# Layer 0 of a fused transformer kernel: the dense pieces of the batches start at slot 13 of the loop in place of slot 1

## The reference, cut to what matters

```python
xn = _layernorm(x, axis=-1)
x = x + _L0_attn_ref(xn, wq, wk, wv, wo) + _L0_ffn_ref(xn, ...)
xn = _layernorm(x, axis=-1)
x = x + _L1_attn_ref(xn, ...) + _L1_ffn_ref(xn, ...)
```

```python
x = fwht(x * SU_ug) / SCALE
x_up = x @ W_up.T * (Wscale_ug[:INTER] * SCALE)          # INTER = 1024
x_gate = x @ W_gate.T * (Wscale_ug[INTER:] * SCALE)
x = silu(x_gate) * x_up
x = fwht(x * SU_dp) / SCALE
x = x @ W_down.T * (Wscale_dp * SCALE)
```

## Time and profile before

| what | us |
|---|---|
| median of 3 runs | 1179.88 (1179.0 to 1183.53) |
| the profiled execution | 1184.52 |
| its span, first to last instruction | 1182.7 |
| PE busy | 1087.1 (92%) |
| DVE busy | 704.8 (60%) |
| ACT busy | 655.8 (55%) |
| POOL busy | 459.1 (39%) |
| mean granted TensorE clock | 0.974 of 2.4 GHz |

### The profile page before, as it was taken

One profiled execution on the slowest core, in us unless ns is written; L12 is line 12 of the kernel. 1 busy time (PEld: TensorE's weight loads), 2 busy tenths in 40 slices (PEclk: granted clock), 3 DMA queues, 4 the chain that ended last, 5 costly groups with the idle time before them and its releaser, 6 DMA issues. The chain is left out here.

```text
span 1182.7 us, 25082 instructions
## 1 busy us (share of the span) xinstructions
PE 1087.1 (92%) x7605; PEld 667.5 (56%) x7606; DVE 704.8 (60%) x2445; ACT 655.8 (55%) x1340; POOL 459.1 (39%) x525
## 2 busy tenths in 40 slices
PE   6679999999999999998879669999999999999985
PEld 3345666666666656663655425555555555555564
DVE  6486656656656666661228836566565656566566
ACT  4214455555555544446243738777877787787720
POOL 4323231322222000000330047777677777777510
PEclk9799999999999999999899979999999999999997
DMA  7500131113111310101110675484557646676277
GB/s 237 98 9 12 30 52 30 31 31 51 31 30 31 48 25 22 22 2 56 36 36 6 166 172 177 142 264 152 179 169 236 191 137 201 189 228 228 76 267 284
DMA packets 81681, 129.65 MB, mean 110 GB/s; under 512 B 32777, under 2 KB 53002, under 8 KB 81035
## 3 DMA queue, kind: packets, MB, share of 16 engines
q1 hardware_dynamic: 61576, 76.94, 23.3%
q0 software_dynamic: 15360, 47.21, 13.0%
q10 hardware_dynamic: 4616, 3.91, 1.2%
HBM read 97.57 MB, written 30.05 MB: 108 GB/s over the span
## 5 line engine op out<-in xcount | busy, mean ns | idle before, releaser
L684 DVE CUSTOM_DVE_ANT_0 a_masked<-a_ps_s,a_mask 128x512 bf16<-128x512 f32 (+3 forms) x512 | 229.9, 487 | 160.4 <-PE a_ps_s L843 156.6
L600 ACT ACTIVATE a_probs<-a_ps_e 128x512 f32<-128x512 f32 (+1 forms) x384 | 188.3, 527 | 122.6 <-PE a_ps_e L863 121.6
L1854 PE MATMUL e_ps_gu<-e_w_gu,e_xT 128*64 x640 | 208.6, 469 | 1.1 <-DVE e_xT L1724 1.1
L189 POOL DMA_INDIRECT yn<-rows,inv x160 | 162.1, 1013 | 122.3 <-DVE inv L1404 60.5
L1854 PE MATMUL e_ps_gu<-e_s_gu,e_xT 128*64 128x352 f32 x640 | 208.6, 469 | 0.0
L1633 POOL DMA_INDIRECT y<-e_y,dst x160 | 161.3, 1008 | 60.5 <-issue 28.9
L1879 PE MATMUL e_ps_y<-e_w_d,e_hT 88*64 x640 | 151.4, 379 | 0.9 <-DVE e_hT L1749 0.9
L1879 PE MATMUL e_ps_y<-e_s_d,e_hT 88*64 88x256 f32 x640 | 151.4, 379 | 0.0
L843 PE MATMUL a_ps_s<-a_kT,a_qT 72*128 72x512 bf16 (+3 forms) x512 | 131.3, 301 | 13.9 <-DVE a_headmax L684 11.1
L860 PE MATMUL a_ps_e<-a_qT,a_kT 75*128 75x512 bf16 (+3 forms) x512 | 140.8, 303 | 2.1 <-ACT a_probs L600 1.8
L1854 PEld LDWEIGHTS e_ps_gu<-e_w_gu,e_xT 128*64 128x64 f32 x640 | 81.7, 137 | 90.6 <-issue 90.6
(11 more groups left out here) (243 smaller groups left out, 1888.6 us busy)
## 6 DMA issues: line engine op xcount, KB each, us to landing
e_w_gu<-e_gu SPq DMA_DIRECT2D x64, 352.0 KB
e_w_d<-e_down SPq DMA_DIRECT2D x64, 176.0 KB
a_qT<-qk_parts SPq DMA_DIRECT2D x48, 192.0 KB
e_w_gu<-y SPq DMA_DIRECT2D x12, 768.0 KB, 6.6
qk_parts<-a_stage SPq DMA_DIRECT2D x16, 256.0 KB, 2.6
e_w_gu<-y SPq DMA_DIRECT2D x4, 1024.0 KB, 7.8
qkv<-y SPq DMA_DIRECT2D x12, 256.0 KB
yn<-rows,inv POOLq DMA_INDIRECT x160, 3.7
```

What stands on the lines that cost most here:

```text
L189: eng.indirect_dma_start(self.x[:, j % self.NS, :], None, t["rows"], bass.IndirectOffsetOnAxis(inv[:, j:j + 1], 0)).then_inc(self.x_in[j % ...
L600: nc.scalar.activation(probs[:, i % HKV, UCOL[u]:UCOL[u + 1]], ps_e[:, (i * 3 + u) % 2, 0:w], ACT.Exp, scale=SCALE0).then_inc(exp_done, 1)
L684: ins = V.tensor_tensor_reduce(masked[:, n % 2, c:c + w], ps_s[:, n % 2, c:c + w], mask[:, T - w:T], 1.0, -3e38, ALU.add, ALU.max, headmax ...
L1854: ins = nc.tensor.matmul(ps_gu[r * SEG:(r + 1) * SEG, j % 2, 0:2 * INTER1], xT[:, j // 2 % 2, j % 2, k * P + r * SEG:k * P + (r + 1) * SEG ...
```

## The change

`FFN0` is the slot of the first dense piece, `NX` the number of `xnT` buffers (2 KB of each partition more). Nothing else differs.

```diff
@@ -202,9 +202,9 @@
         STEPS = HEADS // HKV
         LAG, END = 12, HEADS + 12 + 5
         EARLY, OWN = TPB + 1, TPB
-        FFN0 = 1
+        FFN0 = 13
         HALF = T // 2
-        NQ, NV, NX = 3, 3, 3
+        NQ, NV, NX = 3, 3, 4
         STEPS_R, NS_ = 7, NP_ * 2 + 2
         RQ = MROW + NP_
```

## The result

The changed kernel took 1193.8 us (median of 7 runs, 1189.6 to 1198.0), the kernel before 1183.3 on the same chip (7 runs, 1179.0 to 1185.1). The ratio is 1.0101, 95% interval [1.0081, 1.0121], that is +11.9 us [9.6, 14.3]. Forecast were +8.8 and a ratio of 1.0075, just under the interval: right in direction, too small in size. The profiled execution took 1193.77 (span 1191.9).

The account below looks back on a forecast made before the run. TensorE was busy 92% of the span; VectorE set the pace in slots 2 to 7. Terms −11 + 4.3 + 3.0 − 2.6 + 13.7 + 0.8 + 0.6 = +8.8 us, on 1179.9 giving 1188.7; range 1182.5 to 1196.

Parts of the forecast that it names:

- Head: Slots 1 to 11 lose eleven dense pieces: −11 us, between 13.4 gained at full clock and 8.6 at low clock.
- VectorE sets the pace: Slots 2 to 7 of the old head: VectorE busy 22.1 of 24.0 us, TensorE 17.9.
- Slots 12 to 16: Three more pieces at 2.15 us each, the table load and the clock behind the head: +7.9 us.
- Clock behind the head: Slots 12 and 13 run slow if the clock is low at slot 12: 0 to 2.5 us, taken as +0.6.
- table load: ScalarE's load moves to slot 12's first exponential, where key scores wait: 0 to 1.3 us, taken as +0.8.
- rival 1: The head keeps the full clock, −13.4 there and nothing at slots 12 and 13: +5.8 us, 1185.7; chance 0.27.
- Slots 17 to 127: One piece fewer, fronts in free slots and shorter load waits together: −1.7 us.
- Fronts in free slots: A tile's transpose, parts and projection, formerly behind down slots, now in free ones: +0.7 us each, +3.0 in all.
- load waits: Maximum scores waiting for q and k at slots 32 and 96 get more time: −2.6 us, bounds 0 and −2.6.
- the price of a piece: Two more dense pieces in slots 12 to 127, put at 2.15 us each: +4.3.
- Tail: Nine slots, 128 to 136, go from 2.03 to 3.55 us by a closed gate-up loop: +13.7 us.
- Rivals 2 and 3: First: dearer tail and boundaries, about +15 us, chance 0.16. Second: the tail hides its pieces, +1 us, chance 0.07.

Follow-up runs that it names:

- e6: The changed kernel with idle matmuls that nobody reads at the end of slots 0 to 12 and the table loaded ahead of the loop: 1185.8 us, ratio 1.0045.
- e10: The kernel before with its last dense half at slots 128 to 139 and two of VectorE's down-weight operations moved to ScalarE: 1178.0 us, ratio 0.9962.
- e5: The changed kernel again, unaltered, for more runs and a second profile: 1192.3 us, ratio 1.0099.
- e3: The changed kernel with one exponential ahead of the loop, so that ScalarE loads its table early: 1192.9 us, one run.
- e1: The kernel before with the fourth xnT buffer alone: 1182.6 us, ratio 0.9998.
- e4: The kernel before with only the last dense half moved, from slots 113 to 124 to slots 128 to 139: 1179.2 us, ratio 0.9967.
- e2: The changed kernel with idle matmuls that nobody reads behind the units of slots 0 to 7: 1191.1 us, ratio 1.0075.
- e7: The changed kernel with the first dense piece at slot 9: 1190.0 us, one run.
- e9: The kernel before with the last half at slots 128 to 139, halves 1, 3 and 5 four slots later, and four buffers: 1179.1 us, ratio 0.9969.

## Why the prediction missed the size

- **Head, −11 forecast, −10.8 measured, in part by luck.** VectorE's ten slots from 2 to 12 took 88.75 − 58.20 = 30.55 us, between the 27.4 reckoned for the full clock and the 32.2 for the low one. The reason given was off: I had the clock come back with slots 10 and 11, and it stayed at 0.50 there (slot 11 took 4.22). The low clock cost the head about 3.8 us (slots 2 to 11 took 32.5, and 28.7 with the fillers of e6), not the 2.4 charged; but the gain at the full clock would be about 14.6 (an estimate, 10.8 + 3.8), not 13.4, and the two errors cancel. "VectorE sets the pace" was half the reading (e10), without harm, since the sum took VectorE's own rows.
- **Slots 12 to 16, +7.9 forecast, +7.3 and +9.9 measured. This is the step that failed:** "Clock behind the head, +0.6". It depends on when the clock returns. Slots 12 and 13 took 5.37 us in e6, with the clock at 1.00 (one filler is in them), 6.62 in the first execution, where it returned at 89.8, and 9.18 in e5, where it returned at 96.8. Less 0.4 for the table load, the low clock cost 0.8 and 3.4 us there. The first is near what was charged, the second beyond my upper bound of 2.5.
- **What that explains of +11.9.** With the early return the loop lost 9.6 us, nearly the 8.8 forecast; with the late one it lost 11.7, as much as the medians. The third trace of such a kernel (e3) has the return at 88.9. How often the return is late, and so how much of the gap of 3.1 us between +8.8 and +11.9 is this term, stays open.
- **The clock in all.** Against the full clock I charged 2.4 in the head, 0.6 behind it and 0.8 for the table load, 3.8 in all. By the slots above they cost 3.8, 0.8 or 3.4, and 0.4: 5.0 or 7.6. The medians say 6.5 (e5 against e6), with the fillers' own cost against it. Without these three terms the sum is +5.0 (rival 1, which keeps the table load, is +5.8), and the rest of the measured loops is 9.6 − 5.0 = 4.6 and 11.7 − 7.6 = 4.1. The rest of the sum was right within a microsecond, though single terms in it were not. Rival 1 falls, as the head didn't keep its clock.
- **The clock and gaps.** The clock was granted 0.58 in slots 2 to 7, and 0.50 in slots 8 to 11, where TensorE was busy 9.2 of 11.4 us. The prediction put the new head's gaps at about 1.5 us. The trace has one of 3.73 and one of 2.91 at its start, and the first fall (52.2) lies in the first of them; the second fall (69.3) lies in a gap of 1.76. The Trainium skill ("TensorE: Matmul & The Clock Gate", "Why this matters for your kernels") names long idle gaps between bursts of matmuls as what costs the clock. The trace agrees for the first fall and not for the second.
- **Slots 17 to 127, −1.7 forecast, −0.3 measured.** Fronts in free slots came out, at about 0.55 each (8.96 us for three free slots with a front and 6.57 without, against 13.43 and 11.59 behind down slots) and 0.7 for the last one's parts, 2.9 in all. The load waits went as said, to 0.4 us and none in e5, but their −2.6 is no constant: such waits cost 2.9, 6.6, 4.2 and 2.4 us in before, e1, e4 and e10. They explain part of the difference between executions. What was off is the price of a piece: taking one away here gave back 0.7 us and not 2.15. A piece costs 2.15 in slots 30 and 31 (2.05 and 1.99 without), which gained one, and 1.7 in slots 105 and 106 (4.17 and 3.74 with one), which lost one, so it isn't the same in every place.
- **Tail, +13.7 forecast, +13.4 measured.** Dense tail slots take 3.5 to 3.8 us, by the loop reckoned, and two of the down slots (134 and 135) take 3.2; the mean of the nine is 3.56, where 3.55 was reckoned. Rivals 2 and 3 fall, and no key score waited for the maxima.
- **Table load**, +0.8 forecast, 0.4 measured. **Buffer**, 0 and 0.
- **From the profile to the median.** I subtracted 4.6 us, because the profiled execution lay that far above the median of three runs. 23 runs of the kernel before give 1182.8, so 1.7 of it was warranted. "Its like would take 1193.3" met 1193.8; the 1188.7 was low for this reason too. This doesn't touch the ratio.

Open: why the clock of one program returns at 89.8 in one execution and at 96.8 in another, and why the stage behind the loop, which nothing here touches, varies by 8 us between profiled executions (621.7 in e2 to 629.5 in e7), as much as most effects here.

The best versions, e4, e9 and e10, which can't be told apart, gain 0.3 to 0.4% on the kernel before: it moves only the pieces whose old place (1.83) is dearer than the new (1.6).

## What to carry to other kernels

Price a unit of work at each place it may stand (here 1.0 us per piece in the head, 10.8 / 11, and only 0.45 for the first four; 1.8 among full slots; 1.5 in the tail) before shifting a whole sequence, and move only the units whose old place is the dearer. Here a stretch in which TensorE had little to do lost its clock when it was thinned further, and a part of the bill, 0.8 to 3.4 us, arrived at the first dense work behind it. Look for closed loops through several engines beside the busy shares: VectorE, busy 92% of the stretch, was level with such a loop, and relieving it of 1.22 us in a slot shortened the slot by 0.09.

## What was not expected of the hardware

The clock fell without a long gap. TensorE's timeline of the kernel after, with the gaps around the first fall of the head (52.2) and behind it, then around the second (69.3):

```profile
54.32 0.40 PE L843 MATMUL a_ps_s<-a_kT,a_qT 72*128 72x256 bf16 x1 [3.73 <-DVE a_headmax L684]
...
58.95 0.40 PE L843 MATMUL a_ps_s<-a_kT,a_qT 72*128 72x256 bf16 x1 [2.91 <-DVE a_headmax L684]
...
66.86 0.74 PE L843 MATMUL a_ps_s<-a_kT,a_qT 72*128 72x512 bf16 x3 [0.40 <-DVE a_headmax L684]
69.36 0.39 PE L843 MATMUL a_ps_s<-a_kT,a_qT 72*128 72x256 bf16 x1 [1.76 <-DVE a_headmax L684]
70.05 1.03 PE L843 MATMUL a_ps_s<-a_kT,a_qT 72*128 72x512 bf16 x3 [0.29 <-DVE a_headmax L684]
```

The group took 0.74 us at 66.86 and 1.03 at 70.05, and the idle time between them was 1.76 us at most. The old head's clock fell at 53.1, within the 3.64 of the earlier trace rows. In dense stretches short waits were followed by a low clock too: 1.26 us for q in e1, and 1.70 in e4. Timeline and window of e4:

```profile
169.35 0.39 PE L848 MATMUL a_ps_s<-a_kT,a_qT 72*128 72x512 bf16 x1 [1.70 <-DMA a_qT<-qk_parts]
...
169.70:173.10 3.40, 3.40 (x19) 1.03 (x17) 1.48 (x6) 0.60 (x1) 0.00 (x0) 0.50 0.00 0
```

TensorE is busy for all 3.4 us there, at half clock, and slot 32 took 5.98 us in place of 2.56: 3.4 us for a wait of 1.70. The wait itself is in the view of waits, the other half of the price only in the granted clock. The length of the wait doesn't decide it. Timeline and window of e1, slot 96:

```profile
418.53 0.39 PE L843 MATMUL a_ps_s<-a_kT,a_qT 72*128 72x512 bf16 x1 [2.35 <-DMA a_qT<-qk_parts]
...
418.50:425.00 6.50, 6.47 (x56) 3.77 (x57) 3.82 (x17) 2.46 (x5) 1.40 (x4) 1.00 0.02 5
```

This wait was longer, and the clock stayed at 1.00 behind it, as it did behind the 1.8 us of the earlier trace rows. What decides is open.
